# Gated linear attention inside a three-part layer: output product split into a state part and a local part, and the running state updated right behind the mask

## The reference

```python
q = (x @ W_q).reshape(Bn, Tn, H, dk)          # H = 16 heads, dk = dv = 64
k = (x @ W_k).reshape(Bn, Tn, H, dk)
v = (x @ W_v).reshape(Bn, Tn, H, dv)
a = jax.nn.sigmoid(x @ W_gate + b_gate).reshape(Bn, Tn, H, dk)

def step(S, qkva):
    q_t, k_t, v_t, a_t = qkva
    S = a_t[..., None] * S + k_t[..., None] * v_t[..., None, :]
    o_t = jnp.einsum('bhk,bhkv->bhv', q_t, S)
    return (S, o_t)
```

## Time and profile before

| what | value |
|---|---|
| median of three executions | 2530.24 us |
| lowest and highest | 2522.37 and 2537.93 us |
| the profiled execution: span | 2566.5 us |
| PE busy / DVE busy / ACT busy, share of the span | 82% / 56% / 46% |
| attention, first scores to the last pair | about 792 to 1728 us |

### The profile page before, as it was taken

How to read it: one execution, slowest core, us unless ns; L and a number is a source line. 1 busy time by engine, 2 the same in 40 slices (tenths; PEclk the granted TensorE clock), 3 DMA queues, 4 the chain that set the end, 5 groups by cost and what they waited for, 6 DMA issues and landing times.

```text
span 2566.5 us, 39014 instructions
## 1 busy us (share of the span) xinstructions
PE 2116.7 (82%) x13967; PEld 1819.4 (71%) x13968; DVE 1436.0 (56%) x3544; ACT 1187.6 (46%) x1927; POOL 263.8 (10%) x268
## 2 busy tenths in 40 slices
PE   6079999999958897989888888985199999999780
PEld 5069889888856766666666666765088899988670
DVE  6345554555556675848494848556155545555442
ACT  1056655566535363535353544431166555666330
POOL 1700000000021010000000000003600000000324
PEclk9999999999979999989999999985599999999895
DMA  6322222222220000000000000001411221222214
GB/s 240 134 95 91 90 90 74 63 85 72 83 69 17 1 17 5 14 6 14 6 14 10 9 2 1 1 1 52 169 52 66 90 74 49 86 88 70 85 37 131
DMA packets 95432, 151.14 MB, mean 59 GB/s; under 512 B 9583, under 2 KB 76678, under 8 KB 94068
## 3 DMA queue, kind: packets, MB, share of 16 engines
q1 hardware_dynamic: 83008, 116.46, 13.4%
q0 software_dynamic: 12288, 32.91, 4.1%
HBM read 98.84 MB, written 51.15 MB: 58 GB/s over the span
## 4 chain that ended last, share of the span: by engine, by line
PE 55%; DVE 17%; issue 11%; PEld 7%; POOL 3%; ACT 3%; another core or an unknown queue 1%; SPq 1%; DMA 1%; PEldq 1%; DVEq 0%; POOLq 0%; ACTq 0%
PE bank L545 25%; PE bank L564 11%; PE bank L698 4%; PEld bank L564 3%; PEld bank L545 3%; PE bank L683 3%; PE bank L616 3%; PE bank L686 3%; PE bank L640 3%; DVE wide L1298 2%; DVE wide L1315 2%; DVE wide L1287 2%; DVE wide L1300 2%; DVE temp L1319 2%; DVE halves L1326 2%
## 5 line engine op out<-in xcount | busy, mean ns | idle before, releaser
L545 PE MATMUL bank<-halves 128*128 128x512 f32 (+2 forms) x3744 | 778.6, 368 | 35.5 <-DVE halves L1121 22.3
L545 PEld LDWEIGHTS bank<-halves 128*128 128x128 f32 x3744 | 654.0, 192 | 144.3 <-issue 28.3
L564 PE MATMUL bank<-halves 128*128 128x256 f32 (+1 forms) x3288 | 403.1, 283 | 3.0 <-issue 3.0
L564 PEld LDWEIGHTS bank<-halves 128*128 128x128 f32 (+1 forms) x3288 | 397.3, 189 | 5.7 <-issue 4.8
L801 ACT ACTIVATE temp<-bank,bias_now 128x512 f32<-128x512 f32 (+1 forms) x312 | 200.3, 642 | 389.0 <-PE bank L545 369.6
L1134 DVE SCALAR_TENSOR_TENSOR temp<-bank,bias_fc,temp 128x512 f32<-128x512 f32 (+1 forms) x312 | 216.1, 693 | 247.8 <-ACT temp L801 238.9
L616 PE MATMUL bank<-halves 128*128 128x512 f32 x1152 | 292.6, 406 | 2.0 <-DVE halves L1261 2.0
L1141 DVE TENSOR_TENSOR halves<-temp,halves 128x512 fp32r<-128x512 f32 (+1 forms) x312 | 198.1, 635 | 126.8 <-ACT halves L757 122.0
L616 PEld LDWEIGHTS bank<-halves 128*128 128x128 f32 x1152 | 217.0, 194 | 52.1 <-DVE halves L1261 2.4
L440 POOL DMA_INDIRECT halves<-expert_out,read_slot x96 | 102.9, 1072 | 1284.5 <-DMA expert_out<-rows 654.0
L757 ACT ACTIVATE halves<-temp 128x512 fp32r<-128x512 f32 (+1 forms) x313 | 184.9, 591 | 9.9
(11 more groups left out here) (159 smaller groups left out, 2327.9 us busy)
## 6 DMA issues: line engine op xcount, KB each, us to landing
expert_out<-rows SPq DMA_DIRECT2D x144, 128.0 KB, 1.7
wide<-in_L_ffn_w_c_fc SPq DMA_DIRECT2D x16, 1024.0 KB
wide<-in_L_ffn_w_gate SPq DMA_DIRECT2D x16, 1024.0 KB
wide<-in_L_ffn_w_c_proj SPq DMA_DIRECT2D x16, 1024.0 KB
wide<-expert_in SPq DMA_DIRECT2D x32, 512.0 KB, 4.9
expert_in<-halves SPq DMA_DIRECT2D x9, 1024.0 KB
x<-in_L_attn_x SPq DMA_DIRECT2D x4, 1024.0 KB, 9.5
out_x<-x SPq DMA_DIRECT2D x32, 128.0 KB
```

The lines of the kernel that those rows point to most:

```text
L545: m = pe.matmul(bank[at + b][:, 0:w], a[:, kc, j * P:(j + 1) * P], v[:, kc, 0:w], start=(i == 0), stop=(i == len(ps) - 1))
L564: mm = pe.matmul(bank[4 + t % 2][0:m, 0:C], a[:, j, o:o + m], v[:, j, :], start=(k == 0), stop=(k == len(ps) - 1))
```

## The change

On PE, `scores` is divided into `turn_keys` and `scores`, and `outputs` into `outputs_of_state` (all four products with the incoming state) and `local_outputs` (all eight products with the masked scores). For pair g they now stand as: `turn_keys` of g, `outputs_of_state` of g-1, `scores` of g, `local_outputs` of g-1, `additions` of g. The waits go with their parts: `qk_made` is waited for by `turn_keys`; `ot_split` and `state_ready` by `outputs_of_state`; `prob_made` by `local_outputs`.

On DVE, `chain` of g stands right behind `mask` of g, where before it stood at the start of the next pair, behind `scaled` and `split_o`. The order is now `sum_logs` of g+1, the small work, `mask` of g, `chain` of g, `split_o` of g-1, `scaled` of g+1.

ACT, POOL and the DMA queues keep their streams. No instruction is added or taken away.

```diff
-                def scores(s, g):
-                    G = s * NPAIR + g
-                    pe.wait_ge(qk_made, G + 1)
+                def turn_keys(s, g):
+                    pe.wait_ge(qk_made, s * NPAIR + g + 1)
                     for c in range(SUPER):
                         m = pe.transpose(bank[6][:, c * P:(c + 1) * P], kd[:, c, :], ident[:])
                     m.then_inc(k_turned, 1)
+                def scores(s, g):
+                    G = s * NPAIR + g
                     if g:
                         pe.wait_ge(prob_made, G)
...
-                def outputs(s, g):
+                def outputs_of_state(s, g):
                     G = s * NPAIR + g
-                    pe.wait_ge(prob_made, G + 1)
                     if g:
                         pe.wait_ge(ot_split, G)
                     pe.wait_ge(state_ready, G + 1)
                     for c in range(SUPER):
-                        cols = slice(c * P, (c + 1) * P)
-                        pe.matmul(bank[5][:, cols], state_in[:, c, :], qd[g % 2][:, c, :],
-                                  start=True, stop=False, skip_group_check=True)
+                        pe.matmul(bank[5][:, c * P:(c + 1) * P], state_in[:, c, :], qd[g % 2][:, c, :],
+                                  start=(c == 0), stop=False, skip_group_check=True)
+                def local_outputs(s, g):
+                    pe.wait_ge(prob_made, s * NPAIR + g + 1)
+                    for c in range(SUPER):
                         for h in range(2):
...
-                                          start=False, stop=True, skip_group_check=True)
+                                          start=False, stop=(c == SUPER - 1), skip_group_check=True)
                     m.then_inc(o_done, 1)
...
-                        scores(s, g)
+                        turn_keys(s, g)
                         if g + 1 == NPAIR and not last:
                             turn_x(s + 1)
+                        if g:
+                            outputs_of_state(s, g - 1)
+                        scores(s, g)
                         if g == 0:
                             project_qk(s, 1)
                         else:
-                            outputs(s, g - 1)
+                            local_outputs(s, g - 1)
                         additions(s, g)
...
-                        if g:
-                            chain(s, g - 1)
                         if g + 1 < NPAIR:
                             sum_logs(s, g + 1)
...
                         mask(s, g)
+                        chain(s, g)
+                        if g:
+                            split_o(s, g - 1)
                         if g + 1 < NPAIR:
                             scaled(s, g + 1)
-                            if g:
-                                split_o(s, g - 1)
...
-                    chain(s, NPAIR - 1)
-                    split_o(s, NPAIR - 2)
```

More of the change, by code:

```diff
@@ L681, in outputs @@
                     for c in range(SUPER):
-                        cols = slice(c * P, (c + 1) * P)
-                        pe.matmul(bank[5][:, cols], state_in[:, c, :], qd[g % 2][:, c, :],
-                                  start=True, stop=False, skip_group_check=True)
+                        pe.matmul(bank[5][:, c * P:(c + 1) * P], state_in[:, c, :], qd[g % 2][:, c, :],
[3 more added lines that the diff above has]
+                    for c in range(SUPER):
                         for h in range(2):
-                            m = pe.matmul(bank[5][h * DH:(h + 1) * DH, cols],
+                            m = pe.matmul(bank[5][h * DH:(h + 1) * DH, c * P:(c + 1) * P],
                                           v_sb[:, c, g * P + h * DH:g * P + (h + 1) * DH], prob[h][:, c, :],
-                                          start=False, stop=True, skip_group_check=True)
+                                          start=False, stop=(c == SUPER - 1), skip_group_check=True)
                     m.then_inc(o_done, 1)
@@ L723, in supertile @@
                         project_qk(s + 1, 0)
-                    outputs(s, NPAIR - 1)
+                    outputs_of_state(s, NPAIR - 1)
+                    local_outputs(s, NPAIR - 1)
                     out_projection(s)
```

## The result

The changed kernel takes 2647.5 us (median of 5, 2634 to 2652), the kernel before 2533.8 (median of 5). The ratio is 1.046, with a 95% interval of 1.041 to 1.050: it is slower by 4.6%, 114 us. The forecast was slower, 2745 us with a range of 2650 to 2845; the direction was right and the size was not. The time lies 2.5 us under the range, close to the first rival (2655: the clock costs nothing).

The account below looks back on a forecast made before the run. The prediction took PE and DVE waiting for each other in the attention, 10.47 us per pair, as the bound. It added 125 us for order and 90 for the clock, 215, to the 2530.24 median: 2745 us, range 2650 to 2845.

Parts of the forecast that it names:

- the first rival: Attention: waits on PE do not lower its clock, so only the 125 us of order count; 2655 us, chance 0.16.
- the ring: Attention, PE and DVE waiting for each other: DVE block 7.26 plus PE 5.0 us, 12.3 per pair against 10.47.
- the second ring: DVE and ACT: from `scaled`, 2.76 us to the logarithm plus 2.79 to the mask, 5.55; period 12.85 us.
- the sum: Whole kernel: 125 us from the new order plus 90 us from the clock, 215 us added to the median.
- the first pair: Each supertile's start: the chain waits for the additions, so `qk_made` comes at 1038.3 instead of 1034.2, 11.3 us behind first keys.
- the clock falls: PE in the attention: longer waits before the keys bring many falls to 1.2 GHz, granted clock under 0.96.
- The waits ahead of the keys: PE, before the turned keys: waits for DVE's scaled keys, more than 48 times, 2 to 3 us each.
- the wait of 1.77 us: PE, at pair 6's state before the change: for the first rival, three supertiles have this wait without a fall.
- what the falls cost: PE's part at the lower clock: 0 to 3.3 us per pair, taken as 1.6, 90 us in all.
- the price of PE's part: PE from keys to additions: keys 0.52, scores 1.16, outputs 3.1 whether halved or not, together 4.8 us.
- 0.5 us by which DVE is later: Before the mask: DVE's 5.55 us against PE's 5.0, the slack that could hide a fall of the clock.
- The splitting buys nothing here: PE's outputs: the state part stands behind the same wait that it was to fill, so no gain.

Follow-up runs that it names:

- e1: The changed kernel with DVE's order put back to that of the kernel before (PE's new order alone): 2530.9 us.
- e2: The kernel before with only DVE's new order, PE's order and chunk-by-chunk outputs as before: 2719.3 us.
- e4: The changed kernel with DVE's small work ahead of the scans instead of behind them: 2609.0 us.
- e7: The changed kernel with only the first pair's chain of each supertile left behind `scaled`, as before: 2617.8 us.
- e5: The changed kernel with nine unused filler matmuls on PE ahead of the keys of each pair but the first: 2636.7 us.
- e8: e2 with nine unused filler matmuls on PE ahead of the keys of each pair but the first: 2660.4 us.

## Why the prediction was right in its direction and wrong in its size

**Right: the ring.** Keys wait for `scaled`, `scaled` stands behind the chain, and PE waits in all 56 pairs. e1 and e2 show that DVE's order alone does it.

**Right: the second ring, and its size.** The forecast period for pairs 1 to 3 was 12.85 us; measured 12.84 and 12.85 in the pairs above. The mean stretch from the first to the last keys of a supertile was forecast at 87.6 us without any cost of the clock, and the trace has 87.1, against 72.0 before: 15.0 us more instead of 15.6. Eight times 15.0 is 120 us. Between the supertiles, where the sum had no change, the profiled execution is 11 us shorter than that of before; the medians differ by 114. The sum took all supertiles alike, though the last, without small work for a next one, takes 81.5 us. e4 shows that the wait for the logarithm, with the small work behind it, sets the period.

**Right in the sum, not shown in its price: the first pair.** From the first to the second keys the sum has 11.3 us, 10.6 in the mean, and the trace 10.56. What putting the chain back saves there is 19 us by the keys and 30 by the medians (e7), so the 32 expected of it are not confirmed.

**Right: the clock falls.** The granted clock went from 0.97 to 0.90 in the stretch, and in 42 of the 56 pairs that wait for their keys some of the keys, scores or outputs run at the lower level. The waits ahead of the keys are 3.2 us in the mean, somewhat longer than the 2 to 3 forecast. One argument for the first rival was misread: not three but two of the supertiles without a fall before have the wait of 1.77 us; in the last one no wait for the state is longer than 1.28. Nothing in the sum hangs on it.

**Wrong: what the falls cost.** The term was 1.6 us per pair, 90 us in all; the filler brings back 11 to 16, though it does not remove every fall. The step that failed is the price of PE's part, "one chunk of outputs 0.76, four 3.1, halved or not". It took the chunk of the earlier trace rows, in which state and local products alternate, as the price of any order. Grouped, four state products take 0.98 and eight local ones 0.92 us (e5), 1.9 instead of 3.1. So PE's part is 3.5 us instead of 4.8. The room behind it is 2.0 us in the first pair shown (the 0.44 that is left there and the 1.56 that the fall took), instead of the "0.5 us by which DVE is later". A fall that lengthens PE's part from 3.49 to 5.05 is held by this room, and the period is 12.84 or 12.85 with it or without. In the ungrouped order the room does not hold it; there the clock costs 59 us (e8), and the time is 2719. A second thing was off: 1.6 was a middle between two ends and read from no row, and even in the ungrouped order it is 1.05. The sentence "The splitting buys nothing here" failed with the price: against e2 the grouped outputs are worth 72 us.

## What to carry to other kernels

When two engines wait for each other, write the ring down for the new order as well, and every second ring beside it; a step moved "next to" its input can uncover a wait of a third engine, here ACT's logarithm, that it had been hiding. Small matmuls that alternate between two kinds cost more here than the same ones in groups, so measure a changed interleaving instead of pricing it from the old one. A low clock costs only what the slack does not hold: first find the slack, with all its terms, then price the clock. And try the halves of a change apart: the fastest kernel here, 2480 us, groups the outputs behind the scores and leaves DVE as it was.

## What the runs showed of the hardware

An output block has four fp32 products of 128 x 128 by 128 columns and eight products that fill half of the output partitions each. Chunk by chunk the twelve took 3.0 us (0.76 to 0.79 per chunk, before), and 1.9 us as two groups (0.98 and 0.92, e5), both at the full granted clock. The runs show the gain, not its mechanism.

Nine unused matmuls, 2.2 us together, put ahead of the keys, where the changed kernel waits 2.5 to 5.6 us, raised the mean clock of the attention from 0.90 to 0.95, in the ungrouped kernel from 0.87 to 0.97, and neither kernel became slower.

The same wait is not always followed by a fall: in the kernel before, the outputs behind the keys of pair 6 wait 1.77 or 1.78 us for the state in seven supertiles. In three of them the clock falls behind this wait; in the other four it does not, though in two of these it had fallen one pair earlier.
